# Latent attention in a fused Perceiver layer: the scores of a tile as 64x64 tiles of two heads, row statistics of a step moved to its beginning, weight turns before query turns

## What is computed

```python
def mla(xn, W_kvd, W_qd, W_ku, W_qu, W_vu, W_ropeq, W_ropek, W_o):   # 16 heads of 32
    kv_lat = xn @ W_kvd; q_lat = xn @ W_qd                            # 512 -> 128 each
    k = (kv_lat @ W_ku);  q = (q_lat @ W_qu);  v = (kv_lat @ W_vu)     # 16 + 16 values a head
    q_rope = rotated(q_lat @ W_ropeq); k_rope = rotated(xn @ W_ropek)
    kk = concatenate([k, k_rope]); qq = concatenate([q, q_rope])
    scores = einsum('bqhd,bkhd->bhqk', qq, kk) / sqrt(32)             # 64 x 64 a head
    probs = softmax(causal(scores))
    return einsum('bhqk,bkhd->bqhd', probs, v) @ W_o
x = x + mla(rmsnorm(x, w_ln1), ...)
x = x + moe(rmsnorm(x, w_ln2), ...)      # one shared and seven routed experts, two for each row
```

## Time and profile before

| | |
|---|---|
| median of 3 runs | 841.95 us (841.2 to 843.08) |
| the profiled execution: time, span | 838.71 us, 836.9 us |
| latent attention, first scores to the last output product | 437.1 to 548.2 us |
| granted TensorE clock in this stage | 1.00 (the 2.4 GHz level) |
| busy in the whole span: TensorE, VectorE, ScalarE, GpSimd | 95%, 63%, 37%, 36% |
| from the start of the first maximum of tile 1 to that of tile 5 | 58.38 us |
| after the stage: shared expert, routed experts, last gathers | 548 to 836.9 us |

### The profile page before, as it was taken

One profiled execution on the slowest core, in us unless ns is written; L12 is line 12 of the kernel. 1 busy time (PEld: TensorE's weight loads), 2 busy tenths in 40 slices (PEclk: granted clock), 3 DMA queues, 4 the chain that ended last, 5 costly groups with the idle time before them and its releaser, 6 DMA issues.

```text
span 836.9 us, 16698 instructions
## 1 busy us (share of the span) xinstructions
PE 791.5 (95%) x6401; PEld 580.8 (69%) x6415; DVE 523.1 (63%) x1175; ACT 311.3 (37%) x827; POOL 300.2 (36%) x154
## 2 busy tenths in 40 slices
PE   4899999999899998799999999899999999999996
PEld 3555546554557776677867777688888888888883
DVE  6877977797753447467688878864473443343334
ACT  4322233123353236663158665823313211211211
POOL 0000000000352733434022121343639999994033
PEclk9999999999999999999999999999999999999999
DMA  9968755783520040012159100040375564541147
GB/s 349 379 227 310 272 205 190 281 312 117 215 101 1 1 143 13 1 59 75 51 209 386 61 0 0 2 151 1 151 256 214 184 201 150 174 152 50 56 120 251
DMA packets 46572, 127.00 MB, mean 152 GB/s; under 512 B 4000, under 2 KB 8352, under 8 KB 40368
## 3 DMA queue, kind: packets, MB, share of 16 engines
q1 hardware_dynamic: 36752, 105.44, 34.8%
q10 hardware_dynamic: 7200, 12.32, 4.2%
q0 software_dynamic: 2560, 8.39, 3.1%
HBM read 101.99 MB, written 24.15 MB: 151 GB/s over the span
## 4 chain that ended last, share of the span: by engine, by line
PE 77%; DVE 9%; DMA 5%; ACT 3%; issue 3%; POOL 2%; SPq 0%; ACTq 0%; another core or an unknown queue 0%; DVEq 0%; POOLq 0%
PE scores L592 11%; PE bank L625 9%; PE bank L1126 7%; PE bank L1128 6%; PE bank L1127 6%; DMA nat<-in_ctx_keys 3%; ACT sp L1613 2%; PE bank L805 2%; PE bank L682 2%; PE bank L840 2%; POOL picked L1366 2%; PE bank L684 2%; PE bank L683 2%; PE bank L757 2%; PE bank L870 2%
## 5 line engine op out<-in xcount | busy, mean ns | idle before, releaser
L1812 DVE STREAM_TRANSPOSE ctxT<-nat 128x1024 f32<-128x1024 f32 (+3 forms) x124 | 116.9, 1005 | 2.5 <-DMA nat<-in_ctx_keys 2.0
L625 PE MATMUL bank<-nat,probT 128*64 128x512 f32 (+1 forms) x416 | 94.9, 600 | 0.1
L592 PE MATMUL scores<-ctxT,hn 32*64 32x385 f32 (+5 forms) x2048 | 88.5, 487 | 2.7 <-DVE ctxT L1812 1.9
L1353 POOL TENSOR_TENSOR ring_lo<-ring_raw,ring_hi 128x2048 fp32r<-128x2048 f32 x18 | 83.0, 4611 | 15.2 <-ACT ring_hi L1700 14.0
L1233 POOL TENSOR_TENSOR wq_lo<-wq_raw,wq_hi 128x1024 fp32r<-128x1024 f32 x4 | 9.5, 2414 | 219.8 <-ACT wq_hi L1457 219.8
L592 PEld LDWEIGHTS scores<-ctxT,hn 32*64 32x64 f32 x2048 | 62.6, 131 | 25.6 <-issue 15.4
L1126 PE MATMUL bank<-ring_hi,xg_lo 128*128 x180 | 74.2, 412 | 0.5 <-DVE xg_lo L2435 0.5
L1128 PE MATMUL bank<-ring_hi,xg_hi 128*128 x180 | 70.6, 392 | 0.0
L1127 PE MATMUL bank<-ring_lo,xg_hi 128*128 x180 | 70.1, 389 | 0.0
L625 PEld LDWEIGHTS bank<-nat,probT 128*64 128x64 f32 (+1 forms) x416 | 28.9, 138 | 53.4 <-issue 51.9
L2447 DVE TENSOR_TENSOR rhm_lo<-bank,rhm_hi 128x512 fp32r<-128x512 f32 x21 | 14.5, 692 | 79.6 <-ACT rhm_hi L1711 75.9
(11 more groups left out here) (310 smaller groups left out, 1878.1 us busy)
## 6 DMA issues: line engine op xcount, KB each, us to landing
nat<-in_ctx_keys SPq DMA_DIRECT2D x48, 1024.0 KB, 7.4
ring_raw<-in_Wexp SPq DMA_DIRECT2D x21, 1024.0 KB, 6.1
x_slots<-zeros SPq DMA_DIRECT2D x1, 5632.0 KB, 17.7
y_slots<-zeros SPq DMA_DIRECT2D x1, 5632.0 KB, 32.4
hn<-x_slots ACTq DMA_DIRECT2D x22, 256.0 KB, 4.2
y_slots<-hn ACTq DMA_DIRECT2D x22, 256.0 KB
w_raw<-in_Wexp SPq DMA_DIRECT2D x3, 1024.0 KB, 5.1
nat<-in_ctx_keys SPq DMA_DIRECT2D x16, 130.0 KB
```

The source lines that it names most:

```text
L592: last = nc.tensor.matmul(scores4[64 * b:64 * b + 64, i, 0:keys_in[i]], q4[rows_i, j, 64 * b:64 * b + 64], ctxT[rows_i, b, j, 0:keys_in[i] ...
L625: last = nc.tensor.matmul(bank[7][64 * b:64 * b + 64, :], probT[0:n, j, 64 * b:64 * b + 64], nat[k % 2][0:n, b, j, :], start=j == 0, stop= ...
L1353: last = nc.gpsimd.tensor_tensor(ring_lo[at], ring_raw[at], ring_hi.bitcast(F32)[at], ALU.subtract)
L1812: dve.transpose(dst, src).then_inc(columns_ready, 1)
```

## The change

1. `self_scores` makes all 16 heads of a tile in one place. A matmul is now two heads of one sequence: 64 rows of `qT_h` by 64 queries, against 64 rows of `kT_h` by 128 columns. Sixteen of them fill the two banks; the row half (`r`) decides the bank, the sequence (`b`) the column half. Both masks stand ahead of them, the second behind the wait for the keys, and one `self_full` counts the whole tile instead of one for each half. The exponentials of tile `t - 1` must all be done (`sexp_ready`, `2 t`) before the first mask.
2. `kT_h` has four blocks instead of eight (`KEY_PLACES`); each key copy still moves 32 x 512 values.
3. The scores of tile `k + 1` stand where the first half stood. In step 6 they stand behind `self_output(6)`. Since row half `r` now holds the even or the odd pairs of heads, `self_output` picks `spT` by `QUADS * r + c`.
4. TensorE turns the first probabilities of tile `k` before the queries of tile `k + 1`.
5. VectorE runs `self_norm(k + 3)` and `row_stats(k - 1)` at the beginning of step `k` instead of behind `self_output_out`; `self_norm(3)` goes ahead of the first maximum.
6. In step 6 VectorE copies the output before both maxima of tile 7.

```diff
@@ constants and tiles
-KEY_PLACES = [slice(0, 6, 5), slice(1, 5, 3), slice(2, 8, 5), slice(3, 7, 3)]
+KEY_PLACES = [slice(0, 4, 3), slice(1, 3)]
-        kT_h = [place(88 + 8 * i, f"kT_h{i}", [P, QUADS, 8, SQ]) for i in range(2)]
+        kT_h = [place(88 + 8 * i, f"kT_h{i}", [P, QUADS, 4, SQ]) for i in range(2)]
@@ TensorE
-            def self_scores(t, par, halves):
-                for f in halves:
-                    if not (isinstance(t, int) and t == 0):
-                        pe.wait_ge(sexp_ready, 2 * t + f - 1)
-
-                    nc.tensor.matmul(bank[4 + f][:], ident_bf[:], causal_bf[:].rearrange("p n q -> p (n q)"), start=True,
+            def self_scores(t, par):
+                if not (isinstance(t, int) and t == 0):
+                    pe.wait_ge(sexp_ready, 2 * t)
+                for r in range(2):
+                    if r == 1:
+                        pe.wait_ge(kTh_ready, 2 * t + 2)
+                    nc.tensor.matmul(bank[4 + r][:], ident_bf[:], causal_bf[:].rearrange("p n q -> p (n q)"), start=True,
                                      stop=True)
-                    pe.wait_ge(kTh_ready, 2 * t + 2)
-                    for i in range(2):
-                        for b in range(2):
-                            own = slice(SQ * b, SQ * (b + 1))
-                            last = nc.tensor.matmul(bank[4 + f][own, i * D // 2:(i + 1) * D // 2], qT_h[par][:, 2 * f + i, own],
-                                                    kT_h[par][:, 2 * f + i, 4 * b:4 * b + 4, :].rearrange("p n q -> p (n q)"),
+                for c in range(QUADS):
+                    for b in range(2):
+                        for r in range(2):
+                            own, two = slice(SQ * b, SQ * (b + 1)), slice(SQ * r, SQ * (r + 1))
+                            last = nc.tensor.matmul(bank[4 + r][own, c * P:(c + 1) * P], qT_h[par][two, c, own],
+                                                    kT_h[par][two, c, 2 * b:2 * b + 2, :].rearrange("p n q -> p (n q)"),
                                                     start=False, stop=True, skip_group_check=True)
-                    last.then_inc(self_full, 1)
+                last.then_inc(self_full, 1)
@@ TensorE, self_step
+                if not first:
+                    weight_columns(k, par, 0)
                 if scores:
                     query_columns(k + 1, 1 - par)
-                if not first:
-                    weight_columns(k, par, 0)
...
-                if scores:
-                    self_scores(k + 1, 1 - par, (0,))
+                if scores and project:
+                    self_scores(k + 1, 1 - par)
                 self_output(k, par)
+                if scores and not project:
+                    self_scores(k + 1, 1 - par)
                 if project:
                     from_latents(k + 2, par)
-                if scores:
-                    self_scores(k + 1, 1 - par, (1,))
@@ VectorE
             def self_max(k, par, halves):
                 for f in halves:
-                    dve.wait_ge(self_full, 2 * k + f + 1)
+                    dve.wait_ge(self_full, k + 1)
...
             def self_step(k, par, norm=True, between=(None, None, None)):
                 if not (isinstance(k, int) and k == 0):
+                    if norm:
+                        self_norm(k + 3, 1 - par)
+                        row_stats(k - 1)
                     latents_out(k + 2, par)
...
-                if norm:
-                    self_norm(k + 3, 1 - par)
-                    if not (isinstance(k, int) and k == 0):
-                        row_stats(k - 1)
                 self_inv(k + 1, 1 - par, (0,))
...
+            self_norm(3, 1)
             self_max(0, 0, (0,))
...
+            self_output_out(NT - 2)
             self_max(NT - 1, 1, (0,))
-            self_output_out(NT - 2)
             self_max(NT - 1, 1, (1,))
```

More of the change, by code:

```diff
@@ L946, in self_output @@
                     for i in range(PAIRS):
+                        r, c = i % 2, i // 2
                         at = b * D + i * 2 * HD
[L948 to L950 removed]
+                        last = nc.tensor.matmul(bank[0][SQ * r:SQ * (r + 1), c * P + SQ * b:c * P + SQ * (b + 1)],
+                                                v_own[par][:, at:at + 2 * HD], spT[:, QUADS * r + c, SQ * b:SQ * (b + 1)],
+                                                start=True, stop=True, skip_group_check=True)
                 last.then_inc(yT_full, 1)
@@ L1386, in head_keys_out @@
             rows_h = slice(HD * h, HD * (h + 1))
-            return copy(kT_h[par][rows_h, :, KEY_PLACES[h], :], bank[3][rows_h, :].rearrange("p (c b q) -> p c b q", c=QUADS, b=2))
+            return copy(kT_h[par][rows_h, :, KEY_PLACES[h % 2], :], bank[3][rows_h, :].rearrange("p (c b q) -> p c b q", c=QUADS, b=2))
         @block.scalar
```

5 lines of the change are left out of this document (1 added, 4 removed).

## The result

The changed kernel takes 847.7 us (median of 7 runs, 844.49 to 852.37), the kernel before beside it 841.95 us. The ratio is 1.0061, with a 95% interval from 1.0037 to 1.0084: 3 to 7 us slower. The forecast of 845.6 us has the sign and the place right. One term of its sum is much too small.

A forecast was written before the change was run, and what follows sets the result against it. The prediction took TensorE to bound the loop, with VectorE close behind. Whole-tile wait +0.5, row operations +2.2 and steps 5 to 7 +0.9 gave +3.6 us on 841.95: 845.6 us, range 843.7 to 848, chance 0.62.

The forecast's parts named there:

- What bounds the kernel: Loop: TensorE, busy 13.75 of 14 us, sets the pace; VectorE, busy 11.41, follows closely; a step takes 14.6 us.
- The score tile: Scores on TensorE: new block 0.92 us, 1.1 with changes of tile shape, against 2.2 before; 1.1 us less a step.
- 2.2 before: Time the prediction gave TensorE's two old score blocks in a step, in us, against 1.1 for the new block.
- the rival in which the tiles overlap only two at a time: Score block costs 1.84 us and more; +5.0 us in all, so 850.6 us; chance 0.10.
- The maximum waits for the whole tile: VectorE's first maximum needs all masks and scores: hidden in the loop, +0.5 us in tiles 0 and 1, bounds 0 and 1.2.
- Row operations and GpSimd: Step's beginning: VectorE's scalings wait for GpSimd's instructions, the second ends 3.00 us after the second inverse; +2.2 us over four steps.
- The swap of turns: TensorE's weight turns ahead of query turns: ScalarE's query copy 0.45 us later, but TensorE has time to spare; 0 us.
- the first mask's wait: First mask waits for both rows of exponentials of the tile before, which end well before TensorE gets there; 0 us.
- the smaller key tile: Smaller `kT_h` and its zeroing lie long before and beside other work; 0 us.
- Steps 5 to 7: End of the stage: step 5 gains 0.8 us, step 6 gains 0.6 and loses 2.3; together +0.9 us.
- +2.3 less 0.6: Step 6: `self_output(6)` ahead of tile 7's scores costs +2.3 us; second exponentials following directly save 0.6.
- The sum: Whole kernel: 0.5 + 2.2 + 0.9 = +3.6 us, added to the median of 841.95 us, giving 845.6 us.

The follow-up runs named there:

- both back: Changed kernel with VectorE's row operations behind `y_lo` again and step 6 in the old order: 840.35 us, 0.9981 of the kernel before.
- rows back: Changed kernel with only VectorE's row operations put back behind `y_lo`: 842.84 us, 1.0018 of the kernel before.
- wide tiles: "both back" with scores on 128x64 tiles again, all in one place: 847.25 us, 1.0068 of the kernel before.

## Why the prediction was right, and where it was not

- **What bounds the kernel.** Right: a shorter chain on VectorE left the step of before at 14.68 us. TensorE had not even the gap of 0.25 us that the prediction read in the earlier trace rows; that is a mask without a record. "VectorE has only 2.6 us to spare" counted its busy time, though. Its path through the second maximum had 0.81 us to spare. In "both back" that room is gone, and the ring takes 14.51 us. The forecast did not use it; my expectations for "rows back" and "both back" took TensorE's load for the step, and missed by 0.8 us.
- **The score tile.** Forecast 0.92 us for the block and 1.1 with changes of shape; measured 1.03 start to start, the next block 1.08 where it was 1.03. Against the wide tiles 0.75 us, against both halves of before 0.9 (0.92 + 1.02 - 1.03), not 1.1: the "2.2 before" had the mask's 0.25 us in it, which stays. Two row groups nearly halve it (1.03 for 1.78 us): the rival in which the tiles overlap only two at a time is out.
- **The maximum waits for the whole tile.** Forecast +0.5 us in tiles 0 and 1. Measured +0.25 between them and +0.50 ahead of tile 0, within the bounds. Only half of the 0.50 is the wait: with `self_norm(3)` back behind the maximum it is +0.25 (2.79 us in "both back", 3.04 changed, 2.54 before), and the other half is `self_norm(3)`, which the prediction put at nothing. In the changed kernel's loop the wait cost nothing, as said.
- **Row operations and GpSimd.** Right, and shown by moving one GpSimd instruction. The place that they left was of no use, as said: VectorE now waits 1.22 us there for the first inverse. The second scaling takes 1.50 us, not 1.2 to 1.3, but ends where it should, 3.04 us after the second inverse (3.00 forecast). A step is 15.25 us (15.15 forecast), four steps +2.64 us (+2.2).
- **The swap of turns, the first mask's wait, the smaller key tile.** Zero, the swap as measured.
- **Steps 5 to 7.** Step 5: -0.63 (-0.8 forecast). Step 6 is the term that was mis-sized: "+2.3 less 0.6", that is +1.7, where the trace has +4.10. The order alone costs 1.97 us against before (14.29 to 12.32), near the forecast. The other 2.1 us is the clock, at its 1.2 GHz level through both blocks that I had priced at 2.4 GHz. The prediction took the granted clock of before for granted, and that was 1.00 in the whole stage, though the change put TensorE's blocks of step 6 behind more waiting.
- **The sum.** +3.6 us forecast; from tile 0 to tile 7 it is +6.4 in the profiled execution, of which 2.1 is the clock. The medians, +5.75 us or +5.1 by the ratio, lie between. That is within the range, but the median lies only 0.3 us under its upper end, and the term that brought it there, the clock, was not in the sum: the mechanism in the loop was right, and that the total stayed inside the range is partly luck.

## What to carry to other kernels

The longest wait of an engine need not be where its work counts. Here the 1.48 us of VectorE's wait for the latents were off the ring, and the place behind `y_lo`, where it hardly waited, was on it. Follow the chain round from an instruction to the same one of the next step, over all engines, and compare its length with the load of the bounding engine before counting on the difference. Before moving an instruction of VectorE beside one of GpSimd, look for a row in which the two run together, and count each hand-over between the two, since an instruction of GpSimd behind them takes its turn too. In a stretch with gaps on TensorE, price its blocks at both clock levels. And look at the clocks of all executions before taking the profiled one for typical.

## What was not expected of the hardware

The clock can fall inside a stage whose windows all read 1.00 before. Here it fell after waits of 0.96 and 0.30 us of TensorE and half a us into a third, and it stayed at 0.50 for 6.8 us, for most of which TensorE worked; in another kernel for more than 13 us. Filling one of the gaps moved the fall by 10 us in the profiled execution; in most of the others the mean clock was that of the kernel before.

The statistics instruction (`BATCH_NORM_STATS2`, SBUF to SBUF, 0.69 us) is not held up beside GpSimd's scaling and sum, while the scalings of the same size are, until 0.28 us after GpSimd's end. Here it mattered more which operation was moved than how many.
